# A GRU recurrence on one Trainium2 core: input products in blocks of 24 steps, and extra matmuls on constant operands in every step

## The reference, cut to what matters

```
def cell(h, x):
    gi = x @ W_ih + b_ih
    gh = h @ W_hh + b_hh
    i_r, i_z, i_n = jnp.split(gi, 3, axis=-1)
    h_r, h_z, h_n = jnp.split(gh, 3, axis=-1)
    r = jax.nn.sigmoid(i_r + h_r)
    z = jax.nn.sigmoid(i_z + h_z)
    n = jnp.tanh(i_n + r * h_n)
    h_new = (1.0 - z) * n + z * h
    return (h_new, h_new)
_, hs = jax.lax.scan(cell, initial_state, xs)
```

## Time and profile before

| | |
|---|---|
| median of 3 runs | 2070.93 us (2069.5 to 2075.49) |
| the profiled execution | 2068.51 us |
| its span, first to last instruction | 2066.7 us |
| mean granted TensorE clock over it | 0.873 of full speed |
| TensorE matmuls busy | 1857.9 us (90%), 32542 of them |
| VectorE, ScalarE, GpSimd busy | 1257.9, 1097.8, 377.3 us |

### The profile page before, as it was taken

One profiled execution on the slowest core, in us unless ns is written; L12 is line 12 of the kernel. 1 busy time (PEld: TensorE's weight loads), 2 busy tenths in 40 slices (PEclk: granted clock), 3 DMA queues, 4 the chain that ended last, 5 costly groups with the idle time before them and its releaser, 6 DMA issues. The chain is left out here.

```text
span 2066.7 us, 86137 instructions
## 1 busy us (share of the span) xinstructions
PE 1857.9 (90%) x32542; PEld 1377.3 (67%) x32542; DVE 1257.9 (61%) x5543; ACT 1097.8 (53%) x4105; POOL 377.3 (18%) x1398
## 2 busy tenths in 40 slices
PE   8877998999989989899888899999998999999876
PEld 4234454463644646455556898989898989999875
DVE  5545383654835447363343677777777777777766
ACT  0342736636355363645644565656565655656554
POOL 3000000000000000000000334343434333333335
PEclk7788999999999999999999796969797988879556
DMA  5222213222032220413223000000000000000002
GB/s 175 77 78 53 79 29 94 66 55 87 20 105 56 71 89 1 117 28 73 72 62 108 1 1 0 0 0 0 0 0 0 0 0 0 0 0 0 0 0 82
DMA packets 103527, 86.76 MB, mean 42 GB/s; under 512 B 15616, under 2 KB 90496, under 8 KB 103440
## 3 DMA queue, kind: packets, MB, share of 16 engines
q1 hardware_dynamic: 101392, 84.38, 14.2%
q10 hardware_dynamic: 1664, 1.18, 0.2%
q0 software_dynamic: 384, 0.01, 0.0%
HBM read 60.20 MB, written 21.00 MB: 39 GB/s over the span
## 5 line engine op out<-in xcount | busy, mean ns | idle before, releaser
L1255 PE MATMUL bank_pair_A<-moving,rep 128*128 128x16 f16 x8192 | 327.7, 172 | 55.3 <-DVE moving L1494 49.5
L1255 PEld LDWEIGHTS bank_pair_A<-moving,rep 128*128 128x128 f16 x8192 | 277.8, 99 | 75.6 <-DVE moving L1494 59.1
L1255 PE MATMUL bank_pair_C<-moving,rep 128*128 128x16 f16 x8192 | 321.8, 171 | 0.0
L1255 PE MATMUL bank_pair_B<-moving,rep 128*128 128x16 f16 x8192 | 321.7, 171 | 0.0
L1352 ACT ACTIVATE r_gate<-r_pre 128x16 f32<-128x16 f32 x512 | 110.4, 216 | 301.7 <-DVE r_pre L1443 301.7
L1255 PEld LDWEIGHTS bank_pair_C<-moving,rep 128*128 128x128 f16 x8192 | 266.3, 99 | 0.0
L1255 PEld LDWEIGHTS bank_pair_B<-moving,rep 128*128 128x128 f16 x8192 | 266.3, 99 | 0.0
L1242 PE MATMUL bank_pair_D<-x_part,w_in 128*128 128x256 f16 x1536 | 213.1, 288 | 6.0 <-ACT gi_rz L1379 3.5
L1443 DVE TENSOR_REDUCE r_pre<-bank_pair_A 128x16 f32<-128x32 f32 x512 | 98.1, 192 | 151.5 <-PE bank_pair_A L1255 151.5
L1137 POOL TENSOR_TENSOR x<-x,w_in 128x512 f32<-128x512 f32 x8 | 10.2, 1274 | 964.7 <-DMA w_in<-w_in 964.7
L1043 DVE TENSOR_REDUCE head_max<-bank_pair_A 128x2 f32<-128x1024 f32 x128 | 155.9, 1218 | 38.3 <-PE bank_pair_A L579 38.1
(11 more groups left out here) (260 smaller groups left out, 3632.0 us busy)
## 6 DMA issues: line engine op xcount, KB each, us to landing
rep<-parts SPq DMA_DIRECT2D x256, 64.0 KB
parts<-parts SPq DMA_DIRECT2D x48, 256.0 KB, 2.1
q_rep<-parts SPq DMA_DIRECT2D x32, 256.0 KB, 4.5
k_rep<-parts SPq DMA_DIRECT2D x64, 128.0 KB, 2.8
w_in<-in_x_dram SPq DMA_DIRECT2D x8, 512.0 KB, 4.2
x<-in_x_dram SPq DMA_DIRECT2D x8, 512.0 KB, 4.4
parts<-parts SPq DMA_DIRECT2D x32, 128.0 KB, 2.6
out_dram<-res SPq DMA_DIRECT2D x16, 256.0 KB, 2.1
```

The lines of the kernel that those rows point to most:

```text
L1255: last = nc.tensor.matmul(ps[part][:, o:o + 2 * B], w[:, k, (first + c) * P:(first + c) * P + P], moving[j % 2][:, k, :, :].rearrange("p s ...
```

## The change

Blocks are TS = 24 steps: ten full ones and a last one of 16. Every step of a full block now makes half a product for the next block, so no step is without one: the products are of 192 columns (8 by 24), and of 128 columns where they are for the last block. `x_part` has two halves by parity, and GpSimd splits the next x but one during the first four bodies of a block; the first two blocks' x is split ahead of the recurrence by ScalarE and VectorE. After the eight product matmuls of each step one more matmul of 256 columns is issued (`steady`), on two slices of W_ih, into a PSUM bank that nothing reads. The last 16 steps have eight of these each. GpSimd waits for the evacuation only in the last body of a block. The outer loop goes over pairs of blocks (four times, so it jumps back three times), with the two blocks' code one behind the other, and the last two full blocks and the last 16 steps are written out behind it.

```
+    BODY = 2
+    TS = MC * BODY
+    FULL, LAST = N // TS, N % TS
...
+        x_part = t("x_part", [P, 2, 2, DC, B, TS], F16)
...
+            def run(first, n, parity, made, split):
+
+                steps = first * TS
+                ranges = (((0, DC, split), (DC, RZ, None)) if split else ((0, RZ, None),)) + ((RZ, MC - 1, None), (MC - 1, MC, None))
+                for low, high, piece in ranges:
+                    with eng.Fori(low, high) as m:
+                        for j in range(BODY):
+                            step(steps + m * BODY + j, j, piece and (n + 1, 1 - parity, m, piece))
+                            product(n, parity, m, j, (low >= RZ) + (high == MC), made)
+
+            with eng.Fori(0, (FULL - 2) // 2) as pair:
+                for q in range(2):
+                    run(pair * 2 + q, pair * 2 + (q + 1), 1 - q, TS, TS)
+            run(FULL - 2, FULL - 1, 1, TS, LAST)
+            run(FULL - 1, FULL, 0, LAST, None)
+            with eng.Fori(0, LAST // BODY) as k:
                 for j in range(BODY):
-                    step(k * BODY + (N - TB + j), j, BLOCKS - 1, True)
+                    step(k * BODY + (FULL * TS + j), j)
+                    product(FULL + 1, 1, None, j, False, 0)
...
-            def product(blk, m, j, is_n):
+            def steady(times):
+                for n in range(times):
+                    nc.tensor.matmul(pD[:, 1, 0:2 * P], w_in[0][:, n % DC, 0:P], w_in[1][:, n % DC, 0:2 * P], start=True, stop=True)
+
+            def product(n, parity, m, j, is_n, width):
+                if not width:
+                    return steady(8)
                 if j == 0:
-                    pe.wait_ge(x_lo, blk * DC + DC)
-                    pe.wait_ge(gi_out, blk * MC + m)
+                    pe.wait_ge(x_lo, n * DC + DC)
+                    pe.wait_ge(gi_out, n * MC + m)
                 for k in range(j * DC // BODY, (j + 1) * DC // BODY):
-                    last = products(m, k, pG[0])
+                    last = products(m, k, pG[0], parity, width)
                 if j == BODY - 1:
                     last.then_inc(gi_ps, 1)
+                steady(1)
...
-            for k in range(DC):
-                nc.scalar.activation(x_part[:, 0, k, :, :], xT[:, k, :, 0:TB], ACT.Copy).then_inc(x_hi, 1)
+            for n in range(2):
+                for k in range(DC):
+                    nc.scalar.activation(x_part[:, n, 0, k, :, :], xT[:, k, :, n * TS:(n + 1) * TS], ACT.Copy).then_inc(x_hi, 1)
...
-            def product(blk, m, j, is_n):
-                if j == BODY - 2 and is_n:
+            def product(n, parity, m, j, is_n, width):
+                if j == BODY - 2 and is_n == 2:
 
-                    pool.wait_ge(gi_out, blk * MC + m + 1)
+                    pool.wait_ge(gi_out, n * MC + m + 1)
```

More of the change, by code:

```diff
@@ L1201, in halves, with x_half @@
             return ps.rearrange("p (c s b) -> p c b s", s=2, b=B)
+        def x_half(parity, part, k, width):
+            return x_part[:, parity, part, :, :, :].rearrange("p c b t -> p c (b t)")[:, k, 0:B * width]
         def blocks(eng, step, product):
[L1206 to L1218, removed]
+            def run(first, n, parity, made, split):
[12 more added lines that the diff above has]
+            with eng.Fori(0, LAST // BODY) as k:
                 for j in range(BODY):
-                    step(k * BODY + (N - TB + j), j, BLOCKS - 1, True)
+                    step(k * BODY + (FULL * TS + j), j)
+                    product(FULL + 1, 1, None, j, False, 0)
         @block.sync
@@ L1237, in _, with products, step @@
         def _(pe):
-            def products(m, k, bank):
+            def products(m, k, bank, parity, width):
                 for w in range(2):
                     for part in range(2):
-                        last = nc.tensor.matmul(bank, w_in[w][:, k, bass.ts(m, P)], x_part[:, part, k, :, :].rearrange("p b t -> p (b t)"),
+                        last = nc.tensor.matmul(bank[:, 0:B * width], w_in[w][:, k, bass.ts(m, P)], x_half(parity, part, k, width),
                                                 start=(k == 0 and w == 0 and part == 0), stop=(k == DC - 1 and w == 1 and part == 1))
                 return last
-            def step(step, j, blk, begins=False, k=None):
+            def step(step, j, split=None):
                 pe.wait_ge(seeded, step * 6 + 4)
@@ L1295, in first_products @@
                         pe.wait_ge(x_lo, k + 1)
-                    last = products(m, k, pG[m % 2])
+                    last = products(m, k, pG[m % 2], 0, TS)
                 last.then_inc(gi_ps, 1)
@@ L1520, in _, with split_of @@
         def _(pool):
-            def split(blk, k, j):
-                src = xT[:, bass.ds(k, 1), :, bass.ts(blk, TB)].rearrange("p o b t -> p (o b) t")
-                hi, lo = (x_part[:, n, bass.ds(k, 1), :, :].rearrange("p o b t -> p (o b) t") for n in range(2))
+            def split_of(n, parity, k, width, j):
+                src = xT[:, bass.ds(k, 1), :, bass.ds(n * TS, width)].rearrange("p o b t -> p (o b) t")
+                hi, lo = (x_part[:, parity, part, :, :, :].rearrange("p c b t -> p c (b t)")[:, bass.ds(k, 1), 0:B * width]
+                          .rearrange("p o (b t) -> p (o b) t", b=B) for part in range(2))
                 if j == 0:
```

46 lines of the change are left out of this document (22 added, 24 removed).

## The result

The changed kernel takes 2200.11 us (median of four executions, 2180.92 to 2223.39) against 2070.22 us (2065.32 to 2075.49) for the kernel before in the same comparison: a ratio of 1.0537, 95% interval 1.0492 to 1.0582. It is slower. Its four executions fall into two groups, 2180.92 and 2182.07 us at a mean clock of 0.78 of full speed, and 2223.39 and 2218.14 us at 0.74. The median lies between the groups, and no execution took that time. The execution with the profile is the one of 2180.92 us, with a span of 2179.1.

The account below looks back on a forecast made before the run. TensorE is busy nearly throughout, its clock swinging between half and full in the recurrence. At half clock 875.5 + 87.1 + 55.5 + jumps 4 = 1022 us, +151, and -3 ahead: 2068.5 + 148 = about 2217 us; 8-in-10 range 2008 to 2226.

Parts of the forecast that it names:

- The point: Whole kernel: clock falls at the recurrence's start and stays half until the last 16 steps; about 2217 us, chance 0.35.
- second case at 2176 us: Recurrence: clock falls at the first jump back, step 48, staying half until the last 16 steps; about 2176 us, chance 0.25.
- the lead-in: Ahead of the recurrence: 12 products are shorter, ScalarE has four more copies; -3 us, between -1 and -5.
- two places for the fall: Clock falls at the 1.45 us gap before step 0, a little over one half, or at the outer loop's first jump.
- no way back: Half-clock steps: 1.49 us of wide matmuls in 4.05 doesn't restore the clock; the last 16 steps' 1.71 us does.
- the sizes at half clock: Recurrence steps at half clock, bound by TensorE: 4.05 us in full blocks, 3.63 us with narrow products.
- the jump has to fetch: Outer loop's three jumps back: some 3,400 instructions don't stay in place, so each jump fetches code; the old loop's didn't.
- the jump's price: Outer loop's jumps back: TensorE idle about 1.5 us or more each, from a 1.1 us packet plus 0.41 us.
- the step at full clock: Full-block recurrence step at full clock: TensorE's 3.17 us, just above the chain's 3.14; bounds 3.14 and 3.28.
- held throughout: Rival for the recurrence: the clock stays full throughout, about 2015 us, a gain of 54 us; chance 0.27.
- GpSimd's waits: Recurrence: GpSimd's wait for the evacuation stands once per block, perhaps 0.15 us each, 1.5 us in all.

## Why the prediction was right

The point was 2217 us with a second case at 2176 us; the executions are 2218 and 2223, and 2181 and 2182 us. The median, 2200.11 us, is the time of neither case, and how many of four executions fall into which was chance. That both sums come so near is in part errors that cancel: for 2176 us the jumps cost 5 us more than forecast and the first 48 steps 4.5 more, against 0.9 less in the lead-in and 4.6 less in stages that the sum left alone. By its own steps:

- **Right: two places for the fall.** The start alone was to decide between the two cases, with "a little over one half" for a fall there; it was two of four. Filling the start removed the upper group, 2179 to 2192 us in four of four, and with the start left alone and no jump it was the only place: 2209 to 2211 us in four of four. That both are places of one fall is shown. Whether the 13 matmuls or the wait put ahead of them cures the start was not tried apart. The gap before step 0 is 1.17 us here, not the 1.45 of the earlier trace rows; what decides at the start between one execution and the next is not shown.
- **Right: no way back.** That 1.49 us of wide matmuls in a step of 4.05 does not bring the clock back, and 1.71 in 4.27 does, was inferred from the earlier trace rows, which show only the second. The 168 steps at 4.05 us in the changed kernel, and the return within three or four steps with one more matmul, show it. This was the step on which most hung.
- **Right: the sizes at half clock.** 4.053 and 3.63 us were forecast for steps of full and narrow blocks; the intervals are 4.05 and 3.63. The last 16 steps have three at 4.27 us, then 3.28.
- **Right: the jump has to fetch**, and the old one did not. The traffic, the queue's packets, the idle time that ends with "issue", and its vanishing with shorter code all show it. The Trainium skill (Runtime: NRT & Kernel Launch, "Instruction fetch mechanics") gives TensorE 2048 instructions in place and a stall for a taken branch to what is not there; this trace agrees, with the loop of some 3,400 instructions (the prediction's count) fetched anew in every round, and the same loop with its inner loops merged fetched once (no packet from 1275 to 1760 us). The section has the stall for any branch to what lies outside a window of two pages of 256 instructions; for TensorE this case measures otherwise, since the old loop of some 1,250 instructions is longer than that and was not fetched again.
- **Too small: the jump's price.** The idle time was put at 1.5 us or more, and the three jumps at 6 us in the sum for 2176 (4 in that for 2217). The idle time is 3.73 us at the first jump, the step behind a jump is up to 1 us longer, and the three jumps together are 11 us over normal steps. The prediction priced one packet of q8 and the 0.41 us of a jump to code in place. There is one such packet in the first jump's idle time, and two in the 4.92 us of the kernel with the start filled. The one packet takes 1.3 us. In the traces of these two kernels and of the one with two constant matmuls, at all nine jumps, TensorE's first load comes 1.9 to 2.5 us after the end of the last q8 packet of the idle time; what fills that is not shown, and it is the term that the prediction lacked. ScalarE fetches too, which it had not considered.
- **Too small: the step at full clock.** 3.17 us was the sum for TensorE; the mean of the first 47 is 3.26. The timeline shows why, with TensorE waiting for `moving` in steps that were to be its own. Here one in the first block and one in the second:

```profile
1142.75 0.47 PEld L1263 LDWEIGHTS bank_pair_A<-moving,rep 128*128 128x128 f16 x16 [0.16 <-DVE moving L1512]
...
1217.76 0.47 PEld L1263 LDWEIGHTS bank_pair_A<-moving,rep 128*128 128x128 f16 x16 [0.25 <-DVE moving L1512]
```

  The chain's 3.14 us of the earlier trace rows was one plain step with nothing else on ScalarE and GpSimd. The run with no constant matmul in its product steps shows the chain: TensorE's own sum is 3.06 us there, and at full clock most steps take 3.20 or 3.21 us and a quarter of them 3.31 to 3.42. Whether the evacuation or GpSimd's split lengthens them no run separates. Had the clock held, the kernel would not have been at 2015 us but some 20 higher (an estimate: 240 intervals of 3.26 us, 15 of 3.28 and 11 us for the jumps); the version with short code and one constant matmul has 216 such steps and 2040 us in its best execution, and the fastest version is at 2032. The rival "held throughout" was thus priced too low.
- **Right: the lead-in.** -3 us was forecast between -1 and -5; it is -3.9 (34.3 to 30.4). Not forecast were 2.9 us at the other end, where the clock now enters the last stage at full.
- **Right in the main: GpSimd's waits.** The view of waits has this for the n gate's input after, and in the second group of lines before:

```profile
POOL n_terms L1552 <- ACT gi_n L1395: 56.5, 10, 28.8
```

```profile
POOL n_terms L1533 <- ACT gi_n L1379: 97.6, 29, 32.9
PEld bank_pair_A L1255 <- POOL n_terms L1533: 4.2, 22, 0.2
```

  29 waits of GpSimd became 10, about one for each block, and TensorE's 22 waits behind them are not in the view after, where one in 24 steps had been forecast. With the clock lost it is worth nothing, since TensorE then sets every step.

## What to carry to other kernels

Where a clock is held by how much wide work TensorE has, read from the trace separately what holds it and what brings it back: a change that takes wide work out of every step can pass the first test and fail the second, and then a single gap costs the rest of the stage. Fill the gaps that are known (the start of a serial stage, the way round a loop) and keep a little more work than the least that held it once (all the work added here was constant matmuls of 128 or 256 columns; no run tells whether other work would do); here half a constant matmul more in each step, and two and a half in the narrow block, made 2029 to 2037 us out of 2041 to 2138 at chance. When code of an outer loop grows, look at the instruction queues of all engines, since a fetch on one engine can hide the fetch on another.

## What the runs showed of the hardware

- The fall needs no long gap: the clock went from 1.00 to 0.50 behind idle times of 0.47 us (after step 95, one constant matmul a step), 0.23 us (in the first narrow steps, one) and 0.22 us (about step 26, none). Steps with two held it behind 0.45 us at three jumps, but so did steps with one behind 0.53, in the execution of 2040.87 us: the idle time alone does not decide.
- With the start filled and no fetching jump, the times of one kernel with one constant matmul a step spread from 2041 to 2138 us; with two, and four in the narrow block, they spread by 8 us. Such a spread can itself be a sign of a clock without margin.
- A busy TensorE is not enough: in the 966 us window of the written-out loop its matmul side is busy throughout, and the clock is 0.50.
- A jump back costs TensorE 2.9 to 4.9 us of idle time where its code has to be fetched, and 0.4 to 0.54 us where it is in place. The same jump was 3.73 us in the changed kernel, with one q8 packet, and 4.92 with 13 matmuls more ahead of the loop, with two; why a second was needed was not tried.
